# Table lookups in a cyclic order of buffers, three of eight leaves moved from GpSimd to VectorE, and the first group's preparation moved into the last mix and fold

## What is computed

```python
x = x + attention(layernorm(x), Wq, Wk, Wv, Wo)   # softmax over the 512x512 feature matrix
w = lut[idx]                                      # 16 entries; gate, up: 1376x512, down: 512x1376
x = x + (silu(x2 @ gate.T) * (x2 @ up.T)) @ down.T    # x2 = layernorm(x)
```

## Time and profile before

| | us |
|---|---|
| median of three runs | 1169.69 (1167.72 to 1170.33) |
| the profiled execution | 1168.55 |
| its span, first to last instruction | 1166.7 |
| busy: TensorE / VectorE / ScalarE / GpSimd | 1045.0 / 498.8 / 402.5 / 302.7 |

### The profile page before, as it was taken

The page is one execution under the profiler, slowest core; times in us unless marked ns, Lnnn a source line. Parts: engine busy times, 40 slices in busy tenths (PEclk is TensorE's granted clock), DMA queues, the critical chain, the costliest instruction groups (busy, mean ns, idle before and its releaser), DMA issues.

```text
span 1166.7 us, 13045 instructions
## 1 busy us (share of the span) xinstructions
PE 1045.0 (90%) x4744; PEld 854.8 (73%) x4744; DVE 498.8 (43%) x972; ACT 402.5 (35%) x654; POOL 302.7 (26%) x278
## 2 busy tenths in 40 slices
PE   3978988737677779999999999999999999999997
PEld 3867866525555567888888888888878888888885
DVE  5796889987898532222221312221231223222001
ACT  4876575655555322112212121221212122122111
POOL 4734234455656201111111111121111111111111
PEclk9998989859888888999999999999999999999999
DMA  7851011210000103001000300010030001000000
GB/s 264 264 189 42 22 44 44 107 50 10 10 7 8 36 1 144 1 1 39 35 1 1 145 1 1 1 72 1 1 134 12 1 1 72 1 1 37 1 1 37
DMA packets 25708, 53.47 MB, mean 46 GB/s; under 512 B 2912, under 2 KB 16496, under 8 KB 21296
## 3 DMA queue, kind: packets, MB, share of 16 engines
q1 hardware_dynamic: 20864, 50.47, 11.9%
q10 hardware_dynamic: 4752, 2.16, 0.7%
q0 software_dynamic: 32, 0.01, 0.1%
HBM read 37.89 MB, written 14.75 MB: 45 GB/s over the span
## 4 chain that ended last, share of the span: by engine, by line
PE 61%; issue 1%; DVE 0%; POOLq 0%; POOL 0%; ACT 0%; DVEq 0%
PE bank L840 41%; PE bank L991 18%; PE bank L854 1%; PE bank L887 1%; DVE x1b L1269 0%; POOLq L60 0%; POOL h_lo L599 0%; DVE h_full L1248 0%; ACT h_hi L815 0%; DVEq L60 0%
## 5 line engine op out<-in xcount | busy, mean ns | idle before, releaser
L840 PE MATMUL bank<-x2t_hi,w_hi 128*128 128x512 f32 (+1 forms) x704 | 277.9, 395 | 11.9 <-DVE x2t_lo L1150 7.2
L840 PE MATMUL bank<-x2t_hi,w_lo 128*128 128x512 f32 (+1 forms) x704 | 276.3, 392 | 0.0
L840 PE MATMUL bank<-x2t_lo,w_hi 128*128 128x512 f32 (+1 forms) x704 | 275.6, 392 | 0.0
L1248 DVE TENSOR_TENSOR h_full<-bank,h_gate 128x512 f32<-128x512 f32 (+1 forms) x88 | 60.7, 690 | 472.6 <-PE bank L840 472.5
L599 POOL TENSOR_TENSOR h_lo<-h_full,h_hi 128x512 fp32r<-128x512 f32 (+1 forms) x77 | 99.4, 1290 | 591.7 <-ACT h_hi L815 591.7
L991 PE MATMUL bank<-w_hi,h_hi 128*128 128x512 f32 (+1 forms) x352 | 148.1, 421 | 35.4 <-DVE h_lo L1077 35.4
L840 PEld LDWEIGHTS bank<-x2t_hi,w_hi 128*128 128x128 f32 (+1 forms) x704 | 132.3, 188 | 45.2 <-issue 9.8
L806 ACT ACTIVATE h_gate<-bank 128x512 f32<-128x512 f32 (+1 forms) x88 | 52.4, 596 | 312.2 <-PE bank L840 312.2
L840 PEld LDWEIGHTS bank<-x2t_lo,w_hi 128*128 128x128 f32 (+1 forms) x704 | 131.8, 187 | 30.3
L840 PEld LDWEIGHTS bank<-x2t_hi,w_lo 128*128 128x128 f32 (+1 forms) x704 | 132.2, 188 | 29.7
L991 PE MATMUL bank<-w_lo,h_hi 128*128 128x512 f32 (+1 forms) x352 | 143.5, 408 | 0.0
(11 more groups left out here) (120 smaller groups left out, 1283.0 us busy)
## 6 DMA issues: line engine op xcount, KB each, us to landing
xg<-in_L_attn_x SPq DMA_DIRECT2D x8, 1024.0 KB, 5.7
x1a<-in_L_attn_x SPq DMA_DIRECT2D x4, 1024.0 KB, 4.8
x1b<-in_L_attn_x SPq DMA_DIRECT2D x4, 1024.0 KB, 4.8
out_dram<-x1a SPq DMA_DIRECT2D x4, 1024.0 KB, 3.9
out_dram<-x1b SPq DMA_DIRECT2D x4, 1024.0 KB, 3.9
m_hi<-m_scratch SPq DMA_DIRECT2D x3, 1024.0 KB, 6.4
m_lo<-m_scratch SPq DMA_DIRECT2D x3, 1024.0 KB, 9.7
idx_raw<-in_L_ffn_gate_idx SPq DMA_DIRECT2D x10, 256.0 KB, 5.5
```

What stands on the lines that cost most here:

```text
L840: last = pe.matmul(out_, a, b, start=(i == 0 and j == 0), stop=(i == len(terms) - 1 and j == 2))
L1248: dve.tensor_tensor(h_full[0:n, :], bank[5][0:n, :], h_gate[0:n, :], ALU.mult).then_inc(h_done, 1)
```

## The change

- Leaves: ScalarE makes 0, 3, 2, 5, 6 (was 2, 3, 7, 6), VectorE makes 4, 7, 1 itself (`own_leaf`), GpSimd none. Leaves 1 and 5 (and 6) change their buffer with the parity of u.
- OPS is 10 in place of 11, the order of the merges within a tile is new, and the three masks and the high bit are found in other steps.
- Groups: TURN_V stands behind MIX 0, MIX 1 behind FOLD 0. MIX 1 and FOLD 1 use banks 0 to 3 alone.
- Preparation of the first group: ln1 one tile after each item of MIX 0, turn 0 in FOLD 0, the other turns and attend 0 to 3 between the items of MIX 1, stats2, shift2 and ln2 in FOLD 1; each item has three looks behind it as elsewhere, and the 56 looks of the old preparation are gone: 140 looks (14 tiles) stand ahead of the first FFN and 190 (19 tiles) in it.
- Addresses of the weights, x1a, wa, wb and the result of FOLD 1 move; some waits of `weight_high` go or move; x1a is loaded ahead of the last three raw weights, and no longer behind MIX 1.
- In the Gram phase the index tiles come in the pattern 0, 1, 2, 2 for four token tiles (was 1, 1, 1, 2).

```diff
-    LOOKS_FIRST = 8, 8, 8, 8
-    x1 = [at("x1a", 96, ...
+    x1 = [at("x1a", 48, ...
-    groups = [..., (TURN_V, 0), (MIX, 0), (MIX, 1), (FOLD, 0), (FOLD, 1)]
+    groups = [..., (MIX, 0), (TURN_V, 0), (FOLD, 0), (MIX, 1), (FOLD, 1)]
-    OPS = 11
-    LEAVES = [2, 3, 7, 6]
-    POOL_LEAVES = [0, 1, 5, 4]
-    LEAVES_NEXT = {4: [0], 5: [2, 3], 6: [1, 5], 8: [4]}
-    LEAVES_SAME = {0: [7], 1: [6]}
+    OPS = 10
+    LEAVES = [0, 3, 2, 5, 6]
+    OWN_LEAVES = [4, 7, 1]
+    LEAVES_NEXT = {5: [0], 6: [3], 7: [2], 8: [5]}
+    LEAVES_SAME = {1: [6]}
+            group, m = groups[n // K], n % K
+            if group == (MIX, 0):
+                timeline.append(("first", ("ln1", m)))
+            if group == (FOLD, 0) and m == 1:
+                timeline.append(("first", ("turn", 0)))
+            if group == (MIX, 1):
+                timeline += [("first", ("turn", m + 1))] if m + 1 < T else []
+                timeline.append(("first", ("attend", m)))
+            if group == (FOLD, 1) and m == 0:
+                timeline += [("first", "stats2"), ("rstd", NG)]
+            if group == (FOLD, 1) and m == 1:
+                timeline.append(("first", "shift2"))
+            if group == (FOLD, 1) and m in (1, 2):
+                timeline += [("first", ("ln2", 2 * m - 2)), ("first", ("ln2", 2 * m - 1))]
+            look(LOOKS_TAKE if n < 2 * K else LOOKS_SCORE if is_score(n) else LOOKS_CHAIN, room(n))
+    # sync: ahead of load_raw(WV, 1)
+            sp.dma_start(x1[0][:], xb_dram[0]).then_inc(x_loaded[0], 16)
+    # vector
+            def own_leaf(u, j):
+                tile, high, step, entry = make_leaf(dve, u, j)
+                dve.tensor_scalar(tile, high, step, entry, ALU.mult, ALU.add).then_inc(own_leaf_made, 1)
+                # one tile u; waits left out; '/' is a yield
+                merge(0, r, one) / merge(0, y, z) /
+                own_leaf(u, 4), find_high(u + 1), find_bit(u, 1), find_bit(u, 2) /
+                merge(0, w, five) / own_leaf(u, 7), weight_low(u - 1) / merge(0, one, z) /
+                merge(1, r, y) / merge(1, w, one) /
+                find_bit(u + 1, 0), own_leaf(u + 1, 1) / merge(2, r, w) /
```

More of the change, by code:

```diff
@@ L67, in sem @@
             return ctx.enter_context(nc.semaphore(name))
-        w_at = [12 * c + (8 if c >= 8 else 0) for c in range(C)]
+        w_at = [12 * c + (8 if c >= 4 else 0) for c in range(C)]
         w_hi = [at(f"w_hi{c}", w_at[c], [P, 3, D], F32R) for c in range(C)]
@@ L201, in preln_attention_ghost_ffn @@
         groups = [(GRAM, 0), (GRAM, 1), (PROD, 0), (PROD, 1), (SCORE, 0), (SCORE, 1),
-                  (TURN_V, 0), (MIX, 0), (MIX, 1), (FOLD, 0), (FOLD, 1)]
+                  (MIX, 0), (TURN_V, 0), (FOLD, 0), (MIX, 1), (FOLD, 1)]
         number = {g: q for q, g in enumerate(groups)}
@@ L209, in product_bank @@
         def product_bank(n):
-            return bank[4 * (n // K % 2) + n % K]
+            q = n // K
+            return bank[4 * (q % 2 if q < number[(MIX, 1)] else 0) + n % K]
         def result_of(n):
@@ L218, in result_of @@
             pair = {GRAM: mat_x[b], SCORE: mat_x[b], PROD: mat_y[b], MIX: mat_y[b],
-                    FOLD: (m_hi, m_lo) if b == 0 else wa}[name]
+                    FOLD: (m_hi, m_lo) if b == 0 else mat_x[1]}[name]
             first = gram_first(m) if name == GRAM else 0
@@ L261, in leaf_count, with own_leaf_count, tile_of, leaves_at @@
             return len(LEAVES) * u + LEAVES.index(j) + 1
[L263 to L276, removed]
+        def own_leaf_count(u, j):
+            return len(OWN_LEAVES) * u + OWN_LEAVES.index(j) + (2 if j != 1 else -1)
+        def tile_of(u, j):
+            one, five = (0, 4) if u % 2 == 0 else (4, 0)
+            return picked[u % 2] if j == 0 else part[{1: one, 2: 1, 3: 2, 4: 3, 5: five, 6: one, 7: 2}[j]]
+        def leaves_at(k):
+            u, p = divmod(k, OPS)
+            first = [(0, 0), (0, 3), (0, 2), (0, 5)] if k == 0 else []
+            both = first + [(u, j) for j in LEAVES_SAME.get(p, [])] + [(u + 1, j) for j in LEAVES_NEXT.get(p, [])]
+            return [(v, j) for v, j in both if v < U]
         def make_leaf(eng, u, j):
@@ L318, in room @@
         def room(n):
-            return 15 if n < K * (number[(MIX, 0)] + 1) else 18 if n < K * (number[(FOLD, 0)] + 1) else 24
-        idx_per_tile = [1 + (i % 4 == 3) if i < T * GB else (i >= T * GB + 4) + (i == T * NG - 1) for i in range(T * NG)]
+            return 12 if n < K * (number[(MIX, 0)] + 1) else 15 if n < K * (number[(FOLD, 0)] + 1) else 21
+        idx_per_tile = [(0, 1, 2, 2)[i % 4] if i < T * GB else (i >= T * GB + 4) + (i == T * NG - 1) for i in range(T * NG)]
         assert sum(idx_per_tile) == U
@@ L553, in load_m @@
                     sp.dma_start(flat(half), m_dram[b.half // (GB // 2), i]).then_inc(m_loaded, 16)
-            sp.wait_ge(product_done, K * (number[(MIX, 1)] + 1))
-            load_x(Block(0, 0))
-            for b, pair in enumerate(((m_hi, m_lo), wa)):
+            for b, pair in enumerate(((m_hi, m_lo), mat_x[1])):
                 sp.wait_ge(product_lo, K * (number[(FOLD, b)] + 1))
@@ L679, in turn_first, with normalise @@
                 b = Block(0, 0)
[L680 to L686, removed]
-                    x2_high(b)
+                if step == "x2":
+                    x2_high(b)
+                elif step in ("stats2", "shift2"):
+                    return
+                elif step[0] == "ln1":
+                    if step[1] == 0:
+                        for i in range(4):
+                            act.wait_ge(idx_stored[i], 16 * ((U - 1 - i) // 4 + 1))
+                    normalise(b, xn_first, 0, [step[1]])
+                elif step[0] == "ln2":
+                    normalise(b, xn_first, 1, [step[1]])
                 elif step[0] == "turn":
                     x_high(b, step[1])
-            def normalise(b, into, second):
+            def normalise(b, into, second, tiles=range(T)):
                 scale, bias = rstd[second], shift[second]
@@ L699, in normalise @@
                     act.wait_ge(ln1_stats, b.n - 1)
-                for t in range(T):
+                for t in tiles:
                     act.activation(into[:, t, :], x1[b.parity][:, t, :], ACT.Identity, bias=bias[:, t:t + 1],
@@ L845, in turn_x @@
                 if b.first and t == 0:
-                    pe.wait_ge(product_lo, K * (number[(FOLD, 0)] + 1))
+                    pe.wait_ge(product_lo, K * (number[(TURN_V, 0)] + 1))
                 elif t == 0:
@@ L1112, in look_up @@
                     dve.wait_ge(leaf_made, leaf_count(u, 6))
-                    merge(0, x, z).then_inc(merged, 1)
+                    dve.wait_ge(own_leaf_made, own_leaf_count(u, 7))
+                    merge(0, one, z).then_inc(merged, 1)
                     yield
-                    dve.wait_ge(merged, merge_count(u, M_XZ))
-                    merge(1, w, x).then_inc(merged, 1)
+                    dve.wait_ge(bits_found, 3 * u + 3)
+                    dve.wait_ge(merged, merge_count(u, M_23))
+                    merge(1, r, y).then_inc(merged, 1)
                     yield
-                    if more:
+                    dve.wait_ge(merged, merge_count(u, M_67))
+                    merge(1, w, one).then_inc(merged, 1)
+                    yield
+                    if u + 1 < U:
                         find_bit(u + 1, 0)
+                        own_leaf(u + 1, 1)
                     yield
```

107 lines of the change are left out of this document (36 added, 71 removed).

## The result

The changed kernel takes 1188.76 us (median of four runs, 1187.26 to 1190.42) against 1170.01 for the kernel before in the same set: ratio 1.0164, 95% interval 1.0149 to 1.0179. The forecast was 1157, range 1147 to 1175. The profiled execution has a span of 1188.6 us.

What follows compares the result with a forecast made beforehand. VectorE's decode was taken as the bound: an FFN start at 242 plus 138.2 us puts the last merge at 380.2 for 392.5, so 12.3 us off 1168.55 gives 1156.3, median 1157; range 1147 to 1175.

Steps and rivals of the forecast that it cites:

- rival A: VectorE's own leaf goes one element at a time, 0.60 to 0.66 us; total time 1175 us, slower than before; chance 0.22.
- The bound: VectorE's decode from about 169 to 393 us is the limit; each microsecond the last merge comes earlier saves one in total.
- The leaf: Each of VectorE's three own leaves a tile takes 0.38 us from start to start, bounds 0.14 and 0.66.
- The tile in the FFN: One weight tile on VectorE takes 6.65 us in place of 7.55, bounds 5.9 and 7.5.
- no merge above 0.8: Sign that the forecast is right: no merge in the FFN lasts above 0.8 us.
- No change but some stretching, 1.5 us earlier: Chain up to the last score: three looks an item cost 1.9 us before and 2.0 after; it ends 1.5 us earlier.
- Eight takes at 2.6, FOLD 0 at 186.3: MIX 0 and TURN_V: eight takes from 167.5, 2.6 us each, so FOLD 0 can start at 186.3.
- The FFN 17 us earlier: First FFN starts at 242 in place of 258.8, with 2.7 tiles more to decode in it.
- My sum for the preparation: From 167.5, MIX 0 and TURN_V, FOLD 0, MIX 1, FOLD 1 and x2 added part by part reach the FFN at 242.
- The terms written for FOLD 1: VectorE's add and statistics 1.2, looks 2.0, four takes 10.4, stats2 and shift2 1.7, less 0.4: about 15.5 us.
- Rival C: Preparation between MIX 1's items holds up VectorE and ScalarE at attend; FFN starts at 252, total 1167 us; chance 0.08.
- Rival B: ScalarE's five leaves become the ones waited for, 0.5 us a tile, 12 over 24 tiles; total 1169 us; chance 0.10.

Runs made afterwards that it cites:

- e5: e4 with two constants in place of the leaf's two operands per partition (weights wrong): 1160.42 us, 0.9910 of the kernel before.
- e6: The kernel before, with ScalarE's product copies moved earlier as in e4: 1165.94 us, 0.9965 of the kernel before.
- e8: The kernel before with the new leaf lists alone, plus ScalarE's product copies moved earlier as in e4: 1164.92 us, 0.9952 of the kernel before.
- e3: The changed kernel with ScalarE's leaves two steps later in its list, as they were before: 1183.72 us, 1.0128 of the kernel before.
- e4: The changed kernel with ScalarE's copy of each product up to three looks earlier in its list: 1171.17 us, 1.0024 of the kernel before.
- e2: The kernel before with the new groups, preparation, addresses and index pattern alone, old leaves kept: 1182.94 us, 1.0117 of the kernel before.

## Why the prediction was wrong, point by point

Slower was given a chance of 0.21, nearly all of it for rival A, whose cause did not occur. The last merge came 32.8 us behind the forecast 380.2. Of these, 17.9 had arisen by the first take behind the scores (185.4 for 167.5), 5.6 within the eight takes, 5.5 from there to the first gate, and 3.8 in the FFN.

- **The bound** was right: VectorE's decode sets the last merge, and what lies behind it did not change (last merge to the chain's start, 46.2 us before and 48.1 after, so 1.9 of the 21.9 are there and open).
- **The leaf** was undersized: 0.38 from start to start was taken, 0.46 came (e5: 0.34 and two pointers). 99 x 0.08 is about 8 us. Rival A (0.60 and more) did not happen.
- **The tile in the FFN** was right in kind: one wait for a leaf (3.1 us), 6.9 us for 6.65. Its sign "no merge above 0.8" did not hold by durations (up to 0.88), but from start to start merges stay 0.62 apart. The FFN took 142.0 us for the forecast 138.2.
- **"No change but some stretching, 1.5 us earlier" up to the last score** is the step that failed: it was 15.4 us later (183.7 for 168.3). Two terms are in it. First, I set the three looks at 1.9 us before and 2.0 after. The windows say 126.6 us of work became 135.6. Behind the scores, where the takes can be compared (e6 and e8), three looks take 1.75 with the old leaves and 2.07 with the new. Ahead of the FFN GpSimd's leaves were hardly waited for (2.6 of the 16.7 us of these waits lie before 259), so only stretching could be won there, against three leaves a tile and 8.0 tiles' worth of steps in place of 7.3. Second, ScalarE's list: I checked that each leaf is ready for its merge, and not what stands behind a waiting leaf. The copy of a product did. The change also moved ScalarE's leaves two looks earlier, which the sum does not price; e3 undoes that and gains 5 us. e4 removes the second term (9.4 us up to the last score) and leaves 6.0.
- **Eight takes at 2.6, FOLD 0 at 186.3**: 3.36 apart, at 209.8. The same cause; 2.63 in e4. TensorE was idle for 20.0 us and restarted at matmuls 0.43 apart, as foreseen from the earlier trace rows, but for at least eleven of them (209.8 to 214.6) in place of about eight.
- **The FFN 17 us earlier**: it came at 271.0, 12 later than before, for the reasons above. e2, where only the preparation moves, has it at 243.1. My sum for the preparation held: from the first take behind the scores to the first gate it gave 242 - 167.5 = 74.5, and e4, where the takes have the forecast pace, needs 251.4 - 175.9 = 75.5. (The terms written for FOLD 1 add up to 14.9, not 15.5.) What I left out is that the looks taken out of it have to be done elsewhere, while VectorE is idle for 10 us more ahead of the FFN. By the formula of the prediction with 20.3 tiles at 7.55, e2's last merge comes 243.1 + 153.3 + 10.8 - 392.5 = 14.7 us later than before; it comes 14.2 later. I never worked this out for the preparation by itself.
- **Rival C** (waits at attend, in order, make the FFN late) had the right kind of cause and the wrong place: the waits at the turns are 1.6 us, those at the takes of products (L1195) 30.3. **Rival B** put the waits at the leaves in the FFN, where there were 3.1 us.

## What to carry to other kernels

When two engines walk one list in order, check for each wait that you move not only who waits for its result but what stands behind it in its engine's list; here 0.56 us copies behind waiting leaves cost 16 to 18 us, and moving them cost no instruction. Work moved off a slow engine pays only where that engine was waited for: compare the waits stage by stage before spending the busy engine's time everywhere. And an earlier start of a stage is no gain while the engine that bounds it has the same work to do before the end.

## What the runs showed of the hardware

- The next VectorE instruction starts 0.34 us after the start of a TENSOR_SCALAR from uint8 to float32 of 512 elements with constants (e5), and 0.46 after one with two operands per partition, while it is 0.60 after a float32 subtraction of two tensors.
- In the kernel before all 51 merges longer than 0.9 us (up to 1.2) overlap with an instruction of GpSimd. In e4, where it makes no leaf, five are left, all before 101 us, where GpSimd still has other work, and the longest after 110 us is 0.75: the mean of the merges into `part` fell from 855 ns in the kernel before to 732 in e4.
- Durations alone mislead: in the changed kernel's FFN merges grow from 0.74 us at 270 to 0.86 at 390, and leaves from 0.54 to 0.66; in e4 they stay at 0.72 and 0.53. From start to start it is 0.62 and 0.45 in both, so no time is lost by it. GpSimd is idle there, and what makes them longer is open.
